# Products of a zero tile at the ends, heads and waits of 25 stages of a four-block transformer kernel

## The reference, cut to what matters

```python
x = x + _L0_attn_ref(_layernorm(x), ...)      # causal attention with a bias
x = x + _L0_xattn_ref(ctx_1024, _layernorm(x), ...)
x = x + _L0_ffn_ref(_layernorm(x), ...)
x = x + _L1_attn_ref(_layernorm(x), ...)      # a recurrence, by scans
x = x + _L1_xattn_ref(_layernorm(x), ctx_1024, ctx_1024, ...)  # softmax over heads
x = x + _L1_ffn_ref(_layernorm(x), ...)       # 8 experts, 2 taken
x = x + _L2_attn_ref(_layernorm(x), ...)      # banded attention
x = x + _L2_xattn_ref(_layernorm(x), ctx_1024, ctx_1024, ...)
x = x + _L2_ffn_ref(_layernorm(x), ...)       # 16 experts, 2 taken
x = x + _L3_attn_ref(_layernorm(x), ...)      # retention, gate, small MLP
x = x + _L3_xattn_ref(_layernorm(x), ctx_1024, ...)
x = x + _L3_ffn_ref(_layernorm(x), ...)       # 8-bit tokens, convolution
```

## Time and profile before

| what | us |
|---|---|
| median of 3 runs (2248.95 to 2265.27) | 2252.06 |
| the profiled execution, its own time | 2243.71 |
| its span, first to last instruction | 2241.8 |
| PE busy | 1845.6 (82%) |
| DVE busy | 1481.2 (66%) |
| ACT busy | 1078.9 (48%) |
| POOL busy | 795.1 (35%) |
| mean granted TensorE clock | 0.903 of full |

### The profile page before, as it was taken

One profiled execution on the slowest core, in us unless ns is written; L12 is line 12 of the kernel. 1 busy time (PEld: TensorE's weight loads), 2 busy tenths in 40 slices (PEclk: granted clock), 3 DMA queues, 4 the chain that ended last, 5 costly groups with the idle time before them and its releaser, 6 DMA issues. The chain is left out here.

```text
span 2241.8 us, 32360 instructions
## 1 busy us (share of the span) xinstructions
PE 1845.6 (82%) x11379; PEld 909.1 (41%) x11379; DVE 1481.2 (66%) x2572; ACT 1078.9 (48%) x1949; POOL 795.1 (35%) x680
## 2 busy tenths in 40 slices
PE   5888979999776777777897788999788786899954
PEld 3445423333544444445584552333156534122223
DVE  4544256664565999995435548999654455788676
ACT  3454124545333555552344343888833434266746
POOL 1000025555144999993305012666641312000011
PEclk8899989999887999997897899999979897699967
DMA  6611552210009115003415734331045400444000
GB/s 199 150 40 66 194 185 66 66 34 15 20 26 249 42 24 95 2 1 115 158 58 173 190 83 97 81 72 41 15 157 184 157 10 17 105 111 96 13 1 19
DMA packets 174404, 192.10 MB, mean 86 GB/s; under 512 B 15844, under 2 KB 140335, under 8 KB 173335
## 3 DMA queue, kind: packets, MB, share of 16 engines
q1 hardware_dynamic: 171172, 181.64, 29.5%
q0 software_dynamic: 3072, 8.39, 1.2%
HBM read 125.61 MB, written 68.30 MB: 86 GB/s over the span
## 5 line engine op out<-in xcount | busy, mean ns | idle before, releaser
L3468 POOL TENSOR_TENSOR a2x_masked<-a2x_masked,tall_rows 128x512 f32<-128x512 f32 x128 | 163.2, 1276 | 126.1 <-ACT a2x_masked L3430 126.1
L1561 ACT ACTIVATE experts<-a1x_scores 128x512 f32<-128x512 f32 x256 | 132.2, 602 | 138.2 <-PE a1x_scores L1483 138.2
L3479 DVE TENSOR_REDUCE a3x_row_most<-a3x_ring 128x1 f32<-128x512 f32 x256 | 162.9, 684 | 26.0 <-PE a3x_ring L3318 24.9
L3479 DVE TENSOR_REDUCE a2x_row_most<-a2x_ring 128x1 f32<-128x512 f32 x256 | 162.1, 679 | 4.9 <-PE a2x_ring L3321 4.9
L1598 POOL TENSOR_TENSOR a1x_tree<-experts 128x1024 f32<-128x1024 f32 x64 | 150.6, 2352 | 37.2 <-ACT experts L1561 34.8
L854 DVE TENSOR_REDUCE ctx_then_heads<-a0x_rows 128x2 f32<-128x1024 f32 x88 | 107.7, 1223 | 82.0 <-PE a0x_rows L689 81.8
L671 POOL TENSOR_TENSOR a0x_pair_sums<-a0x_probs_T 128x1024 f32<-128x1024 f32 x48 | 114.7, 2389 | 129.6 <-ACT a0x_probs_T L800 102.2
L1531 DVE TENSOR_REDUCE a1x_most<-a1x_scores 128x128 bf16<-128x2048 f32 x64 | 145.8, 2278 | 14.9 <-PE a1x_scores L1474 14.9
L1522 DVE TENSOR_TENSOR experts<-experts,a1x_inverse_total 128x2048 f32<-128x2048 f32 x64 | 145.5, 2274 | 1.0 <-ACT a1x_inverse_total L1573 1.0
L3423 ACT ACTIVATE a3x_probs_T<-a3x_scores_T 128x1024 f32<-128x1024 f32 x128 | 123.1, 1018 | 46.7 <-PE a3x_scores_T L3345 46.6
L3423 ACT ACTIVATE wide_rows<-a2x_masked 128x1024 f32<-128x1024 f32 x128 | 135.9, 1061 | 1.4 <-POOL a2x_masked L3468 1.4
(11 more groups left out here) (674 smaller groups left out, 4220.3 us busy)
## 6 DMA issues: line engine op xcount, KB each, us to landing
v_scr<-p0x_vout SPq DMA_DIRECT2D x24, 256.0 KB, 2.0
k_scr<-p0x_x SPq DMA_DIRECT2D x24, 256.0 KB, 2.3
ctx_then_heads<-k_scr SPq DMA_DIRECT2D x8, 768.0 KB
a0x_vs<-v_scr SPq DMA_DIRECT2D x8, 768.0 KB, 4.7
experts<-in_L_ffn_w SPq DMA_DIRECT2D x8, 768.0 KB, 6.6
v_scr<-experts SPq DMA_DIRECT2D x16, 256.0 KB, 2.2
a1x_vs<-v_scr SPq DMA_DIRECT2D x16, 256.0 KB, 4.6
v_scr<-m1f_vout SPq DMA_DIRECT2D x16, 256.0 KB, 2.5
```

The lines of the kernel that those rows point to most:

```text
L1561: nc.scalar.activation(ex[:, n % E, 4 * i:4 * i + 4, :], sp_[:, bank(n, i), :, :], ACT.Exp).then_inc(expd, 1)
L3468: nc.gpsimd.tensor_tensor(sm[:, i % 2, 1, :], sm[:, i % 2, 1, :], full[1][:, i // 2 % KT, :], ALU.add).then_inc(pool_masked, 1)
L3479: nc.vector.tensor_reduce(rm[:, u % 2, h * QT + qt:h * QT + qt + 1, part], ring[:, row_place(r) % 3, 0:n], AX.X, ALU.max).then_inc(row_mos ...
```

## The change

A helper issues n products of a new bfloat16 tile of zeros (128 x 512, set once by POOL in the first stage) with the identity, into a bank that nobody reads at that time. They carry no semaphore. Where no free bank was at hand, the stage gets a PSUM tile `spare`. 863 such products are issued in all.

```diff
+        self.zeros = sb("zeros", [P, 512], BF16)
...
+def keep_going(core, bank, n):
+
+    for _ in range(n):
+        core.nc.tensor.matmul(bank, core.ident_bf[:, :], core.zeros[:, :], start=True, stop=True, skip_group_check=True)
...
@@ norm_stage, between the raw and the normed transpositions (media)
+                    keep_going(core, tp[:, 0, :], 9)
...
@@ project_stage, end of PE's list; wait is 28 (p0a), 34 (p1x), 26 (p2a); project_wide_stage has 4
+                keep_going(core, spare[:, :], wait)
...
@@ wide_attention_stage (a0x)
+                keep_going(core, up[:, :], 8)
                 pe.wait_ge(minus_in, 1)
                 done = 0
                 for i in range(NR):
                     row(i)
+                    keep_going(core, up[:, :], 2)
+                keep_going(core, up[:, :], 10)
...
@@ out_norm_stage
                 for t in range(NT - 3, NT if normed_T is not None else NT - 3):
+                    if queries is None:
+                        keep_going(core, spare, 3)
                     turn_normed(t)
...
                         key_product(core, pe, qsems, job, i, q_banks)
+                    keep_going(core, spare, 22)
+                elif normed_T is not None:
+                    keep_going(core, spare, 5)
...
@@ recurrence_stage, end of PE's list
+                keep_going(core, spare[:, :], 52)
...
@@ head_softmax_stage (a1x): before the first scores; then at the last four values
+                keep_going(core, up[:, :, :], 20)
...
+                pe.wait_ge(expd, BANKS * (N - 1))
                 for n in range(N - 4, N):
                     value(n)
+                    keep_going(core, sp_[:, bank(N - 2, 2), :, :], 3)
...
@@ routed_relu_stage (m1f); routed_glu_stage (m2f) has 18 after its router, 22 here, and the same at its tail
                     key_product(core, pe, ksems, job, i, k_banks)
+                keep_going(core, odd_y[:, :], 40)
...
+                pe.wait_ge(y_moved, NJ)
+                keep_going(core, rp[:, :], 12)
                 for t in range(NT):
+                    keep_going(core, rp[:, :], 3)
                     pe.wait_ge(zn_done, t + 1)
...
+                keep_going(core, rp[:, :], 8)
...
@@ ends of gate_stage, dense_turned_stage (d3a) and bit_in_stage: 46, 15 and 45
+                keep_going(core, spare[:, :], 46)
...
@@ quad_attention_stage
                 for r in range(NR):
                     row(r)
+                    keep_going(core, sT[:, 0, 0, :], 1)
                 turn_most(0)
+                if nkey == T:
+                    keep_going(core, sT[:, 0, 0, :], 14)
                 for r in range(NR, lead):
                     row(r)
+                    keep_going(core, sT[:, 0, 0, :], 1)
...
                 value(N - 1)
+                keep_going(core, sT[:, 0, 0, :], 4)
                 turn_u(U - 1)
+                keep_going(core, sT[:, 0, 0, :], 7)
```

More of the change, by code:

```diff
@@ L178, in _ @@
                 end_prefetch(sp, loads, loaded)
+            if tiles_in:
+                @block.gpsimd
+                def _(pool):
+                    nc.gpsimd.memset(core.zeros[:, :], 0.0)
             @block.vector
@@ L232, in _ @@
                     mm.then_inc(raw_turned, 1)
+                if raw_T is not None:
+                    keep_going(core, tp[:, 0, :], 9)
                 for i in range(groups * KH):
@@ L245, in project_stage @@
 def project_stage(core, name, turned_jobs, value_jobs, values="h d", loads=(), first=(), room=None, R=5,
-                  padding=None, rounding=None, early=(), spread=False):
+                  padding=None, rounding=None, early=(), spread=False, wait=28):
     nc = core.nc
@@ L276, in project_stage @@
         vp = st.ps("vp", [P, 3, 512])
+        spare = st.ps("spare", [P, 512])
         V = value_jobs[0][4].shape[-1] if value_jobs else 0
@@ L493, in _ @@
                         value(v)
+                keep_going(core, spare[:, :], 4)
             @block.vector
@@ L1036, in out_norm_stage @@
         np_ = st.ps("norm_T", [P, 2, 512])
+        spare = op[:, 0, :] if queries is not None else st.ps("spare", [P, 512])[:, :]
         aT = st.sb("aT", [P, 2, K, P])
@@ L2234, in _ @@
                 mm.then_inc(counted, 1)
+                keep_going(core, odd_h[:, :], 18)
                 for t in range(NT):
@@ L2244, in _ @@
                     key_product(core, pe, ksems, job, i, k_banks)
+                keep_going(core, odd_h[:, :], 22)
                 pe.wait_ge(ksems.rest, len(key_jobs))
@@ L2297, in _ @@
                     value_product(core, pe, ksems, value_jobs[i], i, v_banks)
+                pe.wait_ge(y_moved, NJ)
+                keep_going(core, op[:, 0, :], 12)
                 for t in range(NT):
+                    keep_going(core, op[:, 0, :], 3)
                     pe.wait_ge(zn_done, t + 1)
@@ L2308, in _ @@
                         value_product(core, pe, ksems, value_jobs[i], i, v_banks)
+                keep_going(core, op[:, 0, :], 8)
             @block.scalar
@@ L2808, in _ @@
                     mm.then_inc(product, 1)
+                keep_going(core, spare[:, :], 15)
             @block.scalar
@@ L2919, in _ @@
                     multiply(i)
+                keep_going(core, spare[:, :], 45)
             @block.scalar
@@ L3780, in program @@
             cross_projections(core, "p1x", wq, wk, wk, core.col("L1_xattn_bq"), core.col("L1_xattn_bk"),
-                              core.row("L1_xattn_bk"), scr, 0.25, values="d h", room=held, R=6, spread=True,
+                              core.row("L1_xattn_bk"), scr, 0.25, values="d h", room=held, R=6, spread=True, wait=34,
                               first=[load for which, part in ((0, 0), (1, 0)) for load in
@@ L3817, in program @@
             self_projections(core, "p2a", wqkv, core.xnT, scr, hd=16, first=quad_loads(bufs, 0, 0, 0, **stack),
-                             padding=(a["mask_BxS2_bf0"], scr["pad_scr"], wide_rows[:, 4096:6144]))
+                             padding=(a["mask_BxS2_bf0"], scr["pad_scr"], wide_rows[:, 4096:6144]), wait=26)
             quad_attention_stage(core, "a2a", T, bufs, v_scr=scr["vs_scr"], ao=ao2a, keys_of=band, queries_of=band,
```

## The result

The changed kernel takes 2261.06 us in the median (2249.62 to 2279.43, 20 runs) against 2252.43 for the kernel before (2244.09 to 2268.56, 20 runs). The ratio is 1.0041, with a 95% interval of 1.0025 to 1.0058: slower by 0.4%, where 1.3% faster was forecast. The profiled execution took 2267.76 us, its span is 2265.9, its mean granted clock 0.950 (0.903 before).

What follows compares the result with a forecast made beforehand. PE was taken as the busiest engine, at half clock for 19% of the span. Gains of 41.8 us less costs of 14.6 gave 27.2 off, from a median of 2252.1 to 2224 us, range 2214 to 2236.

Steps and rivals of the forecast that it cites:

- a3x: Attention stage a3x: 12.9 us of its body at half clock would run at full, a gain of 5.9 us.
- the lead rows run at DVE's pace: In a3x, the 44 lead rows would follow DVE at either clock: no gain, and no cost set against it.
- rival 3: Zero products do not hold the clock, so filled holes overfill and a3x's lead costs 11 us more: 2308 us, chance 0.07.
- Starts bound by PE: Starts of r1a, p1x, p2a, qkv, d3a, m1f and m2f would run at full clock: together 21.3 us gained.
- the chain from there to the scatter and the experts' first load moves with it: 2.8: In m1f, a faster router would move everything up to the experts' first load earlier, gaining 2.8 us.
- Many small ones: First products of nine output stages, parts of a0x, a1x, m1f, m2f, bit_out, media, a2x: together 14.6 us gained, 5 to 20 possible.
- Attention stages: Added products at attention ends cost 2.0 us, in lead rows 1.8 in a2x and 1.5 in a0a and a2a.
- Output stages' 1.15 each: Added products delay o0x, o0f, o1a, o1x and o2x by 1.15 us each; with o0a and o3a, 6.4 us.
- Rival 1: The clock stays up, but PE's gain is mostly not waited for: 5 us off, 2247 us, chance 0.23.
- the first group: Stages that start with PE as the bound, r1a, p1x, p2a, qkv, d3a, m1f, m2f: 21.3 us gained together.
- its bound of 1%: A Trainium skill rule that slow starts cost under 1% of a typical kernel's span, here below 22 us in all.

Runs made afterwards that it cites:

- e1_none: The changed kernel with the helper issuing no products, its zero tile, spare banks and two added waits kept: 2253.65 us, ratio 1.0002 to the kernel before.
- e2: The changed kernel without the one zero product behind each of a3x's 44 lead rows: 2247.14 us, ratio 0.9968 to the kernel before.
- e3: The kernel before with only one zero product behind each of a3x's 44 lead rows: 2279.07 us, ratio 1.0117.
- e7: The changed kernel with the 52 zero products at the end of r1a on 16 of 128 input rows: 2268.36 us, ratio 1.0089 to the kernel before.
- e8: e4_chosen plus two zero products behind each of a3x's 44 lead rows: 2240.86 us, ratio 0.9967 to the kernel before.
- e4_chosen: The changed kernel without zero products in the four quad attention stages and d3a; of output stages only o0f, o1a, o1x, o2x keep them: 2235.61 us, ratio 0.9922.
- e10: e4_chosen with the quad attention stages' zero products back, but none in a3x's lead: 2237.09 us, ratio 0.9943 to the kernel before.
- e11: e4_chosen without the zero products in its four output stages o0f, o1a, o1x and o2x: 2242.92 us, ratio 0.9935 to the kernel before.
- e6: The changed kernel with its zero tile filled with 1.5 and -2.75 in turn: 2264.36 us, ratio 1.0059 to the kernel before.

## Why the prediction was wrong

The sum said 27.2 off (which gives 2224.9, not the 2224 written); the medians say 8.6 on, the profiles of e1_none and of the changed kernel 15.1. By stages, against e1_none:

- **a3x: -5.9 forecast, +21.6 measured.** This term alone is 27.5 us, as much as the whole forecast gain. The step that failed is "the lead rows run at DVE's pace (44 maxima, 25.4 us busy of 27.1) at either clock, no gain", with nothing set against it on the cost side: with the products PE sets the pace, 1.07 us a row at half clock for DVE's 0.61, and the 44 rows take 45.1 us for 27.0. Without these products 14 us of the median come back (e2), and alone they make the kernel before 27 us slower (e3), so this step is what turned a gain into a loss. I had worked out a row for `a2x` (0.65 against 0.61) and not for `a3x`, where I took it that the clock would be at full; the 0.86 at half stood only in rival 3, and the whole case as a last sentence of what would be wrong. Three things failed there. PE that never pauses does not by itself keep the clock up (e7, and the lead itself). A zero product beside a row of 16 input rows costs 0.32 and not 0.216 (e8). And behind a lead at half the body starts at half too: 61 us in all, 20 of them in the body, in place of the 42 that I wanted to save.
- **Starts bound by PE: right in kind in five, not in the tails.** Forecast and measured: `r1a` 2.6 and 2.3, `p1x` 3.1 and 2.9, `p2a` 2.9 and 2.3, `qkv` 2.85 and 2.2, `m2f` 4.9 and 3.1, `d3a` nothing net and 0.4. `m1f` gave 2.8 and 0: its gather starts 4.4 us earlier in the stage (121.2 for 125.6), and the tail takes all of it back. The step "the chain from there to the scatter and the experts' first load moves with it: 2.8" was right up to the gather and failed behind it. That both routed stages fall to half again a few us after their start (0.77 and 0.83 above) was not foreseen either.
- **Many small ones: 14.6 forecast, with bounds of 5 to 20; about 11 read.** `a0x`, `a1x` and the two `b` stages gave 0.9, 1.9 and 1.4 (6.2 forecast). The seven output stages that have the products, without `o2a` and `o3b`, gained 0.8 in all, net of their cost, where I had -1.4; with the forecast 6.4 of costs that is 7.2, and the rest is the 4.2 before it. Nothing is seen of the 2 at the first expert tiles and of `media`'s part of 1.4. `p0a`, which stood in the sum only within a 0.5 for rounding, is 1.8 longer: it lasts 28.1 to 31.4 in the eleven profiles with its 28 products and 27.6 to 27.8 in the three without. The cause was not looked for.
- **Attention stages: 5.3 of costs forecast, 8.8 measured** (`a0a` 4.1, `a2a` 1.7, `a2x` 3.0), though `a0a` moves by chance between 112.5 and 120.0 over profiles that have no product in it. In `a2x`, where e4_chosen and e10 settle it, the price is 5.0 (against e1_none, where `o2a`'s wait ahead of the stage is not filled, it reads 3.0): 2.6 at the lead (1.8 forecast) and 2.4 at the end (0.65), since the end runs at half clock and the zero products with it.
- **Output stages' 1.15 each: right for four** (1.2, 1.2, 1.2 and 1.5 in e11); `o0x`, the fifth, is 2.5 longer than in e4_chosen.
- **The rivals.** Rival 3's premise, zeros, was wrong (e6, and the filled hole ahead of `o1a` at 1.00), but its price for `a3x`'s lead was the one that came. Rival 1, "what PE gains is mostly not waited for", described the rest: without `a3x`'s lead the kernel takes 2247.1, and its number was 2247. That the two agree to the microsecond is luck: it counts half of the first group and of `a3x`, and 14 of costs. Its own evidence, that a filled hole may end too early, played no part in `m1f`, where the 40 products run without a pause up to the experts' first tile. Nor does its bound of 1% stand refuted, as I wrote: 19% of the span was at half clock, but the best kernels gained 0.8 to 0.9%.

The mean clock rose to 0.950, of the forecast 0.97, while the time rose too.

## What to carry to other kernels

In these runs filler on TensorE held the clock where it was of the full 128 input rows and stood in one piece; on 16 rows, or one for one between products of 16 rows, it did not. Ask for each place what the clock did before, what sits next to the filler, and price both at half clock too. Put it only into holes that end in a stage that waits for TensorE, and let it end before the last useful step of another engine: at a barrier an unread product counts like any other. One trace is one execution: what two profiles of the same stage differ by (here 8 us in `m2f` and 7 in `a3x`) is the floor for every small term of a sum.

## What the runs showed of the hardware that I had not expected

**A clock that falls without a pause.** For 5.8 us ahead of the fall at 636.9 in e7, and for the 3.1 us from the start of `a3x` to the fall at 1923.1 in the changed kernel, PE issued without a gap (in the second case the barrier's 1.1 us stand before it). In e4_chosen the body of `a3x` stayed at 0.50 for 30.7 us with PE 29.9 busy, and the same mix of products ran at 1.00 behind it:

```profile
1933.90:1964.60 30.70, 29.90 (x96) 5.46 (x95) 16.71 (x27) 13.10 (x15) 0.00 (x0) 0.50 0.23 42
1964.60:1980.00 15.40, 14.45 (x92) 3.76 (x94) 13.42 (x23) 10.56 (x12) 0.00 (x0) 1.00 0.73 164
```

The Trainium skill (TensorE: Matmul & The Clock Gate, Part 1) explains the gate by how busy TensorE has been; the trace shows that busy in the profile is not enough.

**Signals of PE that arrive late.** In the tail of `m1f` in the changed kernel PE's transposition of `zn` is recorded at 1177.74, and ACT, which waits for nothing else, starts 12 us later. PE's timeline, then ACT's:

```profile
1177.74 0.44 PE L1916 MATMUL m1f_h_T<-ident,m1f_zn 128*128 128x128 f32 x2 [0.29 <-issue]
...
1180.35 0.44 PE L1916 MATMUL m1f_h_T<-ident,m1f_zn 128*128 128x128 f32 x2 [0.66 <-issue]
1190.86 0.80 PE L1643 MATMUL m1f_x_T<-weights,ctx_T 128*128 128x256 f32 x1 [10.07 <-ACT m1f_vout L1655]
```

```profile
1189.74 0.81 ACT L1980 ACTIVATE x_norm_T<-m1f_h_T,feature_columns 128x128 f32<-128x128 f32 x2 [12.04 <-remote]
```

The semaphore's own record stands at 1189.7, about when the last gathered rows landed (1188.5). The same is seen, 5 to 12 us late, while POOL's gather is under way in `m1f` and `m2f` of all twelve experiments, with or without added products, and not once in the profiled execution of before. Of the 12 us by which its `m1f` and `m2f` are shorter than in e1_none, 9 lie behind the start of the gather, where this wait stands (3 lie ahead of it in `m2f`). `m1f`'s gain ends there too: the gather starts 4.4 us earlier than in e1_none and the stage ends no earlier. What holds the signals back I did not find out, nor whether executions that are not profiled have it.
